# Norms of the latents turned and copied in two halves, a quarter of a product behind the transposes, and the mean of the mixed adapters taken later

## What is computed

```python
def _layernorm(x, axis=-1, eps=1e-05):
    m = jnp.mean(x, axis=axis, keepdims=True)
    v = jnp.var(x, axis=axis, keepdims=True)
    return (x - m) / jnp.sqrt(v + eps)

x = x + L0_xattn(layernorm(x), ctx)      # rotary, 32 query heads, 8 of keys
x = x + L0_attn(layernorm(x))            # 32 heads of one token attend to each other
x = x + L0_ffn(layernorm(x))             # three adapters, chosen by row
x = x + L1_xattn(layernorm(x), ctx)      # one head of 512, q and k with an rms norm
x = x + L1_attn(layernorm(x))            # latent attention of low rank
x = x + L1_ffn(layernorm(x))             # eight adapters behind a gate
x = x + L2_xattn(layernorm(x), ctx)      # 32 heads of 16
x = x + L2_attn(layernorm(x))            # latent attention of low rank
x = x + L2_ffn(layernorm(x))             # mixed adapters, below
x = x + L3_xattn(layernorm(x), ctx)      # 32 query heads, 8 of keys, rms norms
x = x + L3_attn(layernorm(x))            # a single head
x = x + L3_ffn(layernorm(x))             # weights from codebooks
```

```python
base = jnp.einsum('bsi,oi->bso', x, W_org)
q = jnp.einsum('bi,ki->bk', x.mean(axis=1), Wq)
scores = jnp.einsum('bk,ek->be', q, lora_keys) / math.sqrt(K)
coeffs = jax.nn.softmax(scores, axis=-1)
h = jnp.einsum('bsi,eir->bser', x, lora_down)
delta = jnp.einsum('be,bser,ero->bso', coeffs, h, lora_up)
return base + delta * (SCALE * MULTIPLIER)
```

## Time and profile before

| | before |
|---|---|
| median of 3 runs | 1639.66 us |
| the profiled execution's own time | 1641.53 us |
| its span | 1639.7 us |
| mean granted clock of TensorE | 0.992 of full speed |
| TensorE, matmuls (PE) | 1529.1 us, 93%, 7405 instructions |
| TensorE, weight loads (PEld) | 1144.4 us, 70% |
| VectorE (DVE) | 1018.2 us, 62%, 2102 instructions |
| ScalarE (ACT) | 874.7 us, 53%, 1603 instructions |
| GpSimd (POOL) | 401.8 us, 25%, 349 instructions |

### The profile page before, as it was taken

How to read it: one execution, slowest core, us unless ns; L and a number is a source line. 1 busy time by engine, 2 the same in 40 slices (tenths; PEclk the granted TensorE clock), 3 DMA queues, 4 the chain that set the end, 5 groups by cost and what they waited for, 6 DMA issues and landing times. The chain is left out here.

```text
span 1639.7 us, 22771 instructions
## 1 busy us (share of the span) xinstructions
PE 1529.1 (93%) x7405; PEld 1144.4 (70%) x7405; DVE 1018.2 (62%) x2102; ACT 874.7 (53%) x1603; POOL 401.8 (25%) x349
## 2 busy tenths in 40 slices
PE   7999999999999988999888888898999999999996
PEld 5878777778784443487466665785777787778874
DVE  3036776766775883275668883663267677676773
ACT  4235665555654441255228885562366667666661
POOL 0001111101111340054327775450011011110131
PEclk9999999999999999999999999998999999999999
DMA  9431222112165007263273421745321122211130
GB/s 323 124 116 59 84 77 75 64 39 79 51 250 204 21 25 256 110 182 123 93 127 46 49 37 53 240 148 212 117 96 56 35 83 77 83 44 46 51 127 14
DMA packets 82088, 167.89 MB, mean 102 GB/s; under 512 B 6768, under 2 KB 48880, under 8 KB 72160
## 3 DMA queue, kind: packets, MB, share of 16 engines
q1 hardware_dynamic: 82016, 166.99, 32.4%
HBM read 142.07 MB, written 17.04 MB: 97 GB/s over the span
## 5 line engine op out<-in xcount | busy, mean ns | idle before, releaser
L2644 POOL TENSOR_TENSOR L2x_p_lo<-L2x_e_t,L2x_p_hi 128x512 fp32r<-128x512 f32 x96 | 122.1, 1294 | 37.7 <-ACT L2x_p_hi L2839 37.6
L736 DVE TENSOR_TENSOR L0x_k_lo<-bank,L0x_k_hi 128x512 fp32r<-128x512 f32 x128 | 85.3, 687 | 53.5 <-ACT L0x_k_hi L638 53.5
L1388 DVE TENSOR_TENSOR L3x_k_lo<-bank,L3x_k_hi 128x512 fp32r<-128x512 f32 x128 | 86.1, 688 | 52.0 <-ACT L3x_k_hi L1280 51.7
L965 POOL TENSOR_TENSOR L3x_v_lo<-L3x_v_raw,L3x_v_hi 128x512 fp32r<-128x512 f32 x32 | 40.5, 1300 | 301.2 <-ACT L3x_v_hi L1271 301.2
L361 POOL TENSOR_TENSOR L0x_v_lo<-L0x_v_raw,L0x_v_hi 128x512 fp32r<-128x512 f32 x32 | 40.5, 1305 | 295.7 <-ACT L0x_v_hi L629 295.7
L638 ACT ACTIVATE L0x_k_hi<-bank 128x512 fp32r<-128x512 f32 x128 | 74.0, 598 | 51.1 <-PE bank L511 50.5
L2893 DVE CUSTOM_DVE_ANT_0 L2x_junk<-bank,L2x_mask 128x512 f32<-128x512 f32 x128 | 86.6, 687 | 23.4 <-PE bank L2732 16.4
L1280 ACT ACTIVATE L3x_k_hi<-bank 128x512 fp32r<-128x512 f32 x128 | 74.1, 605 | 41.4 <-PE bank L1130 41.2
L1377 DVE CUSTOM_DVE_ANT_0 L3x_s<-bank,L3x_mask 128x512 f32<-128x512 f32 x128 | 80.8, 687 | 3.9 <-PE bank L1028 2.0
L725 DVE CUSTOM_DVE_ANT_0 L0x_s<-bank,L0x_mask 128x512 f32<-128x512 f32 x128 | 80.8, 687 | 3.9 <-PE bank L434 2.0
L632 ACT ACTIVATE L0x_s<-L0x_s,L0x_neg_max 128x2048 f32<-128x2048 f32 x32 | 64.3, 2008 | 30.1 <-DVE L0x_neg_max L729 30.1
(11 more groups left out here) (659 smaller groups left out, 4420.1 us busy)
## 6 DMA issues: line engine op xcount, KB each, us to landing
L0x_w_q<-in_L0x_kq SPq DMA_DIRECT2D x8, 1024.0 KB, 5.5
L0x_values<-L0x_v_raw SPq DMA_DIRECT2D x32, 256.0 KB, 2.2
L0x_w_o<-in_L0x_o SPq DMA_DIRECT2D x8, 1024.0 KB, 4.8
L0x_v_raw<-L0x_values SPq DMA_DIRECT2D x8, 1024.0 KB, 4.8
L1a_w_o<-in_L1a_o SPq DMA_DIRECT2D x8, 1024.0 KB, 6.6
L2a_w_o<-in_L2a_o SPq DMA_DIRECT2D x8, 1024.0 KB, 7.1
L3x_w_q<-in_L3x_kq SPq DMA_DIRECT2D x8, 1024.0 KB, 5.3
L3x_w_o<-in_L3x_o SPq DMA_DIRECT2D x8, 1024.0 KB, 4.7
```

The source lines that it names most:

```text
L736: dve.tensor_tensor(p_lo[:, kt % 4, :], ring_bank(kt)[:], bits(p_hi[:, kt % 4, :]), ALU.subtract).then_inc(p_ready, 1)
L1388: dve.tensor_tensor(p_lo[:, kt % 4, :], ring_bank(kt)[:], bits(p_hi[:, kt % 4, :]), ALU.subtract).then_inc(p_ready, 1)
L2644: pool.tensor_tensor(p_lo[:, t % 8, :], e_of(t), bits(p_hi[:, t % 8, :]), ALU.subtract).then_inc(low_pool, 1)
```

## The change

It has five parts.

1. The norm turns blocks 0 and 1 into one bank and blocks 2 and 3 into a second one (bank 7; in L1a, L2a and L3a bank 5, in L3f bank 2). VectorE copies each with an instruction of 256 columns, and counts `ready` up to 2. `tensor` no longer waits for the copies. Instead `wait_turned` stands ahead of the matmul that first reads block 0 and of the one that first reads block 2.
2. In L0f, L1x, L1a and L1f the first tile of values is made up to its third quarter ahead of the transposes, and the last quarter behind them. The same is done with tile 10 around the transposes of q in L1x, and with tile 7 around the transposes of o in L0a.
3. In L2x the transposes stand ahead of the last of the four chunks of narrow keys.
4. In L2f the first quarter of the hidden product (four matmuls) comes ahead of the product of the mean.
5. In L0x and L3x `project_q` waits for `ready` at 2 in each of its sixteen calls, and GpSimd in L2x as well as VectorE in L2f wait for 2 where they waited for 1.

The diff, cut to its core (`...` marks what is left out):

```diff
@@ -166 @@
 
-    def __init__(self, core, st, bank):
-        self.core, self.bank = core, bank
+    def __init__(self, core, st, bank, second):
+        self.core, self.bank, self.second = core, bank, second
         self.xn = st.sb("ln_xn", [P, D])
...
@@ -189 @@
             meanwhile()
-        dve.wait_ge(self.turned, 1)
-        dve.tensor_copy(core.xn_t[:], self.bank[:].rearrange("p (c q) -> p c q", c=CT)).then_inc(self.ready, 1)
+        for i, bank in enumerate((self.bank, self.second)):
+            dve.wait_ge(self.turned, i + 1)
+            dve.tensor_copy(core.xn_t[:, 2 * i:2 * i + 2, :],
+                            bank[:, 0:2 * P].rearrange("p (c q) -> p c q", c=2)).then_inc(self.ready, 1)
 
...
@@ -206 @@
         pe.wait_ge(self.xn_ready, 1)
-        for c in range(CT):
-            mm = pe.transpose(self.bank[:, c * P:(c + 1) * P], self.xn[:, c * P:(c + 1) * P], self.core.ident[:])
-        mm.then_inc(self.turned, 1)
-        pe.wait_ge(self.ready, 1)
+        for i, bank in enumerate((self.bank, self.second)):
+            for j in range(2):
+                c = 2 * i + j
+                mm = pe.transpose(bank[:, j * P:(j + 1) * P], self.xn[:, c * P:(c + 1) * P], self.core.ident[:])
+            mm.then_inc(self.turned, 1)
+
+    def wait_turned(self, pe, c):
+        if c % 2 == 0:
+            pe.wait_ge(self.ready, c // 2 + 1)
 
...
@@ -265 @@
         core.memory.take_again(lent)
-        norm = LayerNorm(core, st, core.bank[0])
+        norm = LayerNorm(core, st, core.bank[0], core.bank[7])
         w_hi = st.sb("w_hi", [P, CT, HD], F32R)
...
@@ -450 @@
                     pe.wait_ge(w_q_in, g * 16 + 16)
+                    pe.wait_ge(norm.ready, 2)
                     for h in range(HG):
...
@@ -1677 @@
                     for c in range(CT):
+                        if j == 0:
+                            norm.wait_turned(pe, c)
                         mm = pe.matmul(core.bank[j][:], core.xn_t[:, c, :], w[:, c, j * D:(j + 1) * D],
...
@@ -1693 @@
                         values.tensor(pe, i, tile_bank(i), part=(kt - 11) % 2, parts=2)
-                values.tensor(pe, 7, tile_bank(7))
+                for part in range(3):
+                    values.tensor(pe, 7, tile_bank(7), part=part, parts=CT)
                 pe.wait_ge(o_ready, 1)
                 o_flat = o_sb[:].rearrange("p h e -> p (h e)")
                 for c in range(CT):
                     mm = pe.transpose(core.bank[3][:, c * P:(c + 1) * P], o_flat[:, c * P:(c + 1) * P],
                                       core.ident[:])
                 mm.then_inc(o_turned, 1)
+                values.tensor(pe, 7, tile_bank(7), part=3, parts=CT)
                 pe.wait_ge(o_t_ready, 1)
...
@@ -1858 @@
             def _(pe):
-                values.tensor(pe, early, tile_bank(early))
+                for part in range(3):
+                    values.tensor(pe, early, tile_bank(early), part=part, parts=CT)
                 norm.tensor(pe)
+                values.tensor(pe, early, tile_bank(early), part=3, parts=CT)
                 pe.wait_ge(w_in, 32)
                 for c in range(CT):
+                    norm.wait_turned(pe, c)
                     mm = pe.matmul(core.bank[1][:, 0:WIDE], core.xn_t[:, c, :], w[:, c, D:],
...
@@ -1992 @@
                 pe.wait_ge(w_in, 48)
-                pe.wait_ge(mean_ready, 1)
-                for c in range(CT):
-                    mm = pe.matmul(core.bank[1][:, 0:1], w[:, c, 2 * D:], mean[:, c:c + 1], start=(c == 0),
-                                   stop=(c == CT - 1))
-                mm.then_inc(q_ready, 1)
                 for t in range(CT):
+                    if t == 1:
+                        pe.wait_ge(mean_ready, 1)
+                        for c in range(CT):
+                            mm = pe.matmul(core.bank[1][:, 0:1], w[:, c, 2 * D:], mean[:, c:c + 1], start=(c == 0),
+                                           stop=(c == CT - 1))
+                        mm.then_inc(q_ready, 1)
                     for c in range(CT):
+                        if t == 0:
+                            norm.wait_turned(pe, c)
                         mm = pe.matmul(core.bank[3][:, t * P:(t + 1) * P], w[:, c, D + t * P:D + (t + 1) * P],
...
@@ -2022 @@
                 steps = Steps(dve, own)
-                dve.wait_ge(norm.ready, 1)
+                dve.wait_ge(norm.ready, 2)
                 steps.then(dve.tensor_reduce(mean[:], core.xn_t[:], AX.X, ALU.add))
...
@@ -2389 @@
             def _(pe):
-                values.tensor(pe, 9, tile_bank[9])
+                for part in range(3):
+                    values.tensor(pe, 9, tile_bank[9], part=part, parts=CT)
                 norm.tensor(pe)
+                values.tensor(pe, 9, tile_bank[9], part=3, parts=CT)
                 pe.wait_ge(w_in, 16)
                 for c in range(CT):
+                    norm.wait_turned(pe, c)
                     mm = pe.matmul(core.bank[2][:], core.xn_t[:, c, :], w[:, c, :], start=(c == 0),
                                    stop=(c == CT - 1))
                 mm.then_inc(q_proj, 1)
-                values.tensor(pe, 10, tile_bank[10])
+                for part in range(3):
+                    values.tensor(pe, 10, tile_bank[10], part=part, parts=CT)
                 pe.wait_ge(q_ready, 1)
                 for c in range(CT):
                     mm = pe.transpose(core.bank[3][:, c * P:(c + 1) * P], q_sb[:, c * P:(c + 1) * P], core.ident[:])
                 mm.then_inc(q_turned, 1)
+                values.tensor(pe, 10, tile_bank[10], part=3, parts=CT)
                 pe.wait_ge(q_t_ready, 1)
...
@@ -2624 @@
                 pool.wait_ge(mask_ready, 1)
-                pool.wait_ge(norm.ready, 1)
+                pool.wait_ge(norm.ready, 2)
                 pool.memset(bits(q_sc[0][:]), 0.0)
...
@@ -2702 @@
                     mm.then_inc(k_proj, 1)
-                norm.tensor(pe)
+                    if n == NC - 2:
+                        norm.tensor(pe)
                 for h in range(HG):
                     for c in range(CT):
+                        if h == 0:
+                            norm.wait_turned(pe, c)
                         mm = pe.matmul(core.bank[5][:, h * P:(h + 1) * P],
...
@@ -3125 @@
                 for i in tiles[0:1]:
-                    values.tensor(pe, i, tile_bank(i))
+                    for part in range(3):
+                        values.tensor(pe, i, tile_bank(i), part=part, parts=CT)
                 if not tiles:
                     norm.keep_clock(pe)
                 norm.tensor(pe)
+                for i in tiles[0:1]:
+                    values.tensor(pe, i, tile_bank(i), part=3, parts=CT)
                 pe.wait_ge(w_a_in, 16)
                 for c in range(CT):
+                    norm.wait_turned(pe, c)
                     mm = pe.matmul(banks[0][:, 0:QR + KR + RD], core.xn_t[:, c, :], w_a[:, c, :], start=(c == 0),
```

22 lines of the change are left out of this document (13 added, 9 removed).

## The result

| | before | changed |
|---|---|---|
| median of 7 runs, same chip | 1643.40 us | 1634.13 us |
| lowest, highest | 1639.43, 1644.62 | 1630.09, 1634.96 |
| ratio, 95% interval | | 0.9946 [0.9930, 0.9962] |

The changed kernel is faster by 8.9 us (the ratio times the time before), between 6.2 and 11.5. The forecast was 13.2 us and 1626.5 us, with a range of 1621.5 to 1632.0. The direction was right, the size was too large, and the time lies outside the range. The 1639.66 us from which the forecast subtracted was the median of three runs; four more on the same chip gave 1643.40 to 1644.62. Of the 7.6 us by which the median misses the forecast, 3.7 are this base and 3.9 are gain that did not come (13.2 less the 9.3 between the medians).

The account below looks back on a forecast made before the run. TensorE, busy 93% of the span, bounds the kernel, so its idle or half-clock time counts. Gains of 2.00 + 5.64 + 0.31 + 0.86 + 4.37 = 13.18 us give 1626.5 us, range 1621.5 to 1632.0.

Parts of the forecast that it names:

- The quarter behind the transposes: L0f, L1x, L1a, L1f, L2x: moved work keeps TensorE busy behind the norm's transposes, saving 0.94 us per stage.
- The halves: L0a, L2a, L3a, L3f: two half-width copies let the first reader start after 0.88 instead of 1.38 us, saving 0.50 each.
- The end of L0a: Tile 7's last quarter fits whole into the 1.46 us wait behind the transposes of o, saving 0.86 us.
- q in L1x: Moving a quarter of tile 10 behind q's transposes lets them start earlier, saving 0.31 us.
- the order of L2f: L2f: eight of the 32 hidden product instructions run before the mean's product, saving 0.88 us.
- the waits of project_q: L0x and L3x: sixteen added waits cost 0.3 us at most, taken as nothing.
- TensorE waiting for both copies: Norms with halves: bound of 0.09 us gain each if TensorE waits for both copies; counted within rival 3, chance 0.09.
- the swallowed gains: Rival 3: chains not starting at TensorE swallow half of the 8.8 us gained outside L2f, giving 1630.9 us; chance 0.09.
- Rival 1: The clock falls in L2f all the same, so 3.40 us stay: 1629.9 us; chance 0.13.
- L2x and L3x: Norms of L2x and L3x: the empty stretch behind the transposes goes, saving 0.94 us in each.
- 3.40 us are the clock's: L2f, transposes to base product: 3.40 of 7.94 us are lost to half clock, and the changed order regains them.
- rival 2: Other clock dips, in L1a and L2a, vanish as work moves, saving 1.5 and 1.7 us: 1623.3 us; chance 0.15.

Follow-up runs that it names:

- held pair: Kernel before and changed kernel, each with unused dummy products ahead of TensorE's idle waits (27 and 26 places): medians 1635.16 and 1624.78 us.
- undo_l2f_2: Changed kernel with only L2f's order put back (mean's product first), a repeat; mean 1633.8 us over fourteen executions of both batches.
- pure delay: Kernel before with nine dummy products behind the norm's wait in L0a, all later work 2 us later: ratio 1.0016 [1.0001, 1.0030].

## Why the forecast came out as it did

**Right.** The terms that count instructions and empty stretches. Without the clock they say 9.78 us; the held pair gives 10.2 (9.9 without the dummies ahead of L2f's mean) and the line at equal clock 10.6. That the sum fits so well is in part luck, as L2x gave 0.64 too little and L3x 0.46 too much. The quarter behind the transposes was worth 1.05 us against 0.94: the 0.11 more is the first weights, loaded ahead. The halves were worth 0.41 us against 0.50. I had taken both durations from L0f, but in L0a, L2a, L3a and L3f the old distance from first transpose to first reader is 1.42 to 1.44 us, and the new one 1.02 to 1.05 instead of 0.88, since the first copy starts 0.45 to 0.48 after the first transpose (0.41 in the forecast) and the reader 0.57 after that (0.47). The end of L0a, q in L1x, the order of L2f (0.95 us between undo_l2f_2 and the changed kernel, 17.23 and 16.28, against 0.88) and the waits of project_q (nothing) came as worked out. "TensorE waiting for both copies" and the swallowed gains did not happen. Two copies take 0.84 us of VectorE (2 x 0.42) where one took 0.69, and nothing waited for the 0.15 us. The Trainium skill (VectorE: DVE Perf Modes, the trn2 errata) names that fixed cost per instruction; its heading speaks of sources in SBUF, but its table has a fixed term for reads out of PSUM too, as here. The trace agrees with it (0.15 us), and it lay under matmuls. Rival 1 did not come either: L2f stood at 1.00 in all eight profiles with the changed order, five without dummies near it and three of held kernels. By what the Trainium skill says of transposes (TensorE: Matmul & The Clock Gate, Part 4) it could have; these profiles neither need that rule nor refute it.

**Partly wrong: L2x and L3x.** The queries of L2x did start 0.94 us earlier in the held pair, but 0.3 us of it went at the stacked queries, behind GpSimd's maxima, and 0.34 at 173 us of the stage's 215, behind VectorE's low part. L3x gave 0.46 more than its 0.94: 0.11 at the first values matmuls, and 0.35 ahead of the last output product, unforeseen and unexplained.

**Wrong: the step "3.40 us are the clock's".** As a reading of the profiled execution it was nearly right: the fall cost 3.25 us there (20.64 less 17.39), and the order and the second copy brought 1.11 where 0.97 was expected, so that 4.37 came out to the hundredth by luck. It was also right that the changed order holds the clock. The mistake was to book what one execution lost as what the kernel loses, and to leave the clock of all other places out of the sum. With the mean's product first, and no dummies ahead of it, the clock fell in L2f in 5 of 9 profiles, which makes the term about 1.8 us, an estimate from six kernels (3.25 x 5/9). In the means the edit was worth 4.5 us alone on the kernel before, about what was booked, but only 1.1 in the changed kernel, where it was to be added to the other parts (standard errors 0.9).

**Wrong: the chance of rival 2.** It had the mechanism, that other stretches come or go when the work moves, and said that one can come newly behind the pause between L1f and L2x, where one did (in one of three profiles). But it stood at 0.15 and only in the direction that helps. Over 18 executions the mean clock is 0.9912, not above 0.9919. At 1.32 us per 0.001 the clock thus took 0.9 us (standard error 0.5) where it was to give 3.4. By the profiles, of the 4.3 us between, 1.6 are L2f's (3.4 less 1.8) and 2.7 other places'. By the kernels with one part, L2f's order gave 2.8 us of clock, the halves took 2.5 and the quarters 1.1, together 0.8 lost against the 0.9 of the changed kernel; each of the three has a standard error of 0.7 to 0.9 us. Against it stand 0.8 us that the rest gave more than its 9.78. So 13.2 became 9.6 us in the means.

**Wrong: the base and the range.** Three runs within 0.6 us looked like a sharp time. The program spreads over 11 us, and its mean is 2.7 us above that median. The range of 10 us held only my uncertainty on the change.

**Open.** That the halves alone run at 0.990 repeated and isn't explained. Nor is it settled why the means of the changed kernel, with L2f held, don't lie above those of before. If the three parts' effects on the clock simply added up, undoing L2f's order in the changed kernel should have cost 2.8 us of clock, and it cost none that can be seen. The pure delay shows that the places also occur without the change, and the small gains may only make the thin stretches meet the falls more often; no run here separates that.

## What to carry to other kernels

A stretch at half clock in one profile is a possible loss, not a fixed one: read two or three profiles of the same kernel, book it by how often it comes, and allow for other places that the rest of the edit may bring. Compare kernels at equal mean clock to see what an edit did, and by their means to see what it is worth. Filling TensorE's waits near thin work with dummy products, in 26 or 27 places, was worth 6.8 us on the kernel before and 7.4 on the changed one, beside 9.6 for all the moves, and it made most stages of single profiles comparable to a tenth of a microsecond (L0a, 0.8 off in one, shows that not all).

## What was unexpected of the hardware

The granted clock fell at different places in executions of one and the same program (684 us, or not; L2x for 6.83 or 13.65 us), and it did so or not after an idle time of TensorE of the same 1.80 us. With the old order it fell in L2f exactly in those profiles in which it had fallen 17.07 us before, at the end of L2a. About 200 short extra instructions on TensorE (7615 and 7603 against 7405) made the kernels faster: 1642.3 to 1635.5 us and 1632.7 to 1625.3 us in the means.
